# First self attention's scores as three 16 bit products instead of one 32 bit product, with new orders of the first and middle rounds, in a fused attention and feed-forward kernel on one Trainium2 core

## The reference, cut to what matters

```python
def _attention(q_in, k_in, v_in, WQ, WK, WV, causal):
    Q = einsum('bse,ed->bsd', q_in, WQ); K = einsum('bse,ed->bsd', k_in, WK); V = einsum('bse,ed->bsd', v_in, WV)
    scores = einsum('bqd,bkd->bqk', Q, K) / sqrt(d)       # causal: masked above the diagonal
    return einsum('bqk,bkd->bqd', softmax(scores), V)
...
a = _attention(inputs, inputs, inputs, Wq, Wk, Wv, causal=True) + inputs   # the "first attention"
h = _layer_norm(a, gamma, beta)
c = _attention(h, context, context, Wcq, Wck, Wcv, causal=False) + h       # over 257 context rows
h = _layer_norm(c, gamma, beta)
f = relu(einsum('bse,ed->bsd', h, W1) + b1)
return relu(_layer_norm(f + h, gamma, beta))
...
x = x + xattn(layernorm(x), ctx)          # block 1
x = x + attn16heads(layernorm(x))         # block 2
x = x + ffn(layernorm(x))                 # block 3: a gated feed-forward, and experts for some rows
```

## Time and profile before

| | us |
|---|---|
| median of 3 runs (1462.0 to 1462.47) | 1462.03 |
| the profiled execution's own time | 1461.23 |
| its span, first to last instruction | 1459.4 |
| PE busy | 1369.7 (94%) |
| DVE busy | 1128.3 (77%) |
| ACT busy | 588.8 (40%) |
| POOL busy | 529.0 (36%) |
| mean granted TensorE clock | 0.992 |
| a round in the middle (the same unit of one tile and the next, 703.08 to 743.92) | 40.84 |

### The profile page before, as it was taken

The page is one execution under the profiler, slowest core; times in us unless marked ns, Lnnn a source line. Parts: engine busy times, 40 slices in busy tenths (PEclk is TensorE's granted clock), DMA queues, the critical chain, the costliest instruction groups (busy, mean ns, idle before and its releaser), DMA issues.

```text
span 1459.4 us, 32980 instructions
## 1 busy us (share of the span) xinstructions
PE 1369.7 (94%) x13732; PEld 857.8 (59%) x13733; DVE 1128.3 (77%) x2334; ACT 588.8 (40%) x1115; POOL 529.0 (36%) x545
## 2 busy tenths in 40 slices
PE   7679999999999999999999999999999999999888
PEld 3345566666566666666666666656656566655443
DVE  5776687777887777777878778777778778777876
ACT  2543334344444444433444444444344444433232
POOL 0133334344343334434443333434433333433222
PEclk9899999999999999999999999999999999999999
DMA  9723444333334444323334444323323444323540
GB/s 349 256 82 122 145 146 141 112 112 127 110 128 146 145 146 145 127 99 131 112 115 145 146 146 146 136 100 121 131 102 139 146 145 146 142 87 152 191 176 30
DMA packets 38660, 201.39 MB, mean 138 GB/s; under 512 B 5096, under 2 KB 5992, under 8 KB 28400
## 3 DMA queue, kind: packets, MB, share of 16 engines
q1 hardware_dynamic: 37648, 198.93, 38.2%
q10 hardware_dynamic: 864, 0.36, 0.1%
HBM read 182.24 MB, written 17.04 MB: 137 GB/s over the span
## 4 chain that ended last, share of the span: by engine, by line
PE 70%; DVE 19%; ACT 4%; POOL 4%; issue 3%; DMA 0%; DVEq 0%; POOLq 0%; ACTq 0%; SPq 0%
PE ps_a L1703 11%; PE ps_a L1726 8%; PE ps_t L1726 8%; PE ps_a L1712 6%; PE ps_t L1690 6%; PE ps_a L1767 4%; PE ps_a L1738 4%; PE ps_v L1703 4%; PE ps_t L1703 3%; DVE stats L1165 3%; POOL rstd L629 3%; DVE arena L1296 3%; PE ps_t L1738 2%; PE ps_t L1759 2%; PE ps_t L1810 2%
## 5 line engine op out<-in xcount | busy, mean ns | idle before, releaser
L638 POOL TENSOR_TENSOR act_l<-act_t,act_h 128x512 f16<-128x512 f32 (+1 forms) x176 | 199.2, 1132 | 383.8 <-ACT act_t L782 221.9
L629 POOL TENSOR_TENSOR rstd<-var,mhalf 128x1 f32<-128x1 f32 x224 | 185.5, 828 | 302.8 <-DVE var L1167 302.7
L638 POOL TENSOR_TENSOR last_slot<-last_slot 128x512 f16<-128x512 f32 x80 | 89.5, 1119 | 167.7 <-ACT last_slot L782 96.8
L774 ACT ACTIVATE act_h<-ps_t,scale 128x512 f16<-128x512 f32 (+1 forms) x110 | 70.8, 643 | 156.2 <-PE ps_t L1690 156.2
L1726 PE MATMUL ps_a<-act_h,arena 128*128 128x128 f16 x1408 | 87.5, 221 | 18.0 <-ACT act_h L774 18.0
L1726 PEld LDWEIGHTS ps_a<-act_h,arena 128*128 128x128 f16 x1408 | 81.8, 99 | 28.3 <-ACT act_h L774 22.3
L1726 PE MATMUL ps_t<-act_h,arena 128*128 128x128 f16 x1408 | 88.0, 222 | 4.5 <-ACT act_h L774 4.5
L1726 PEld LDWEIGHTS ps_t<-act_h,arena 128*128 128x128 f16 x1408 | 82.4, 99 | 6.1 <-issue 2.9
L1703 PE MATMUL ps_a<-arena,act_h 128*128 128x512 f16 x352 | 83.4, 380 | 1.6 <-ACT act_h L774 1.6
L782 ACT ACTIVATE act_t<-ps_t,scale 128x512 f32<-128x512 f32 (+1 forms) x110 | 70.2, 639 | 34.9 <-PE ps_t L1690 34.9
L1296 DVE TENSOR_SCALAR arena<-ps_a,unscale 32x512 f32<-32x512 f32 x64 | 48.3, 754 | 43.7 <-PE ps_a L1738 42.5
(11 more groups left out here) (369 smaller groups left out, 3087.7 us busy)
## 6 DMA issues: line engine op xcount, KB each, us to landing
arena<-in_ctx_t SPq DMA_DIRECT2D x32, 2056.0 KB, 8.4
arena<-in_ctx_n SPq DMA_DIRECT2D x32, 2048.0 KB
ctx_last<-in_ctx_last SPq DMA_DIRECT2D x32, 256.0 KB
arena<-in_ew SPq DMA_DIRECT2D x8, 1024.0 KB, 6.2
x_in<-in_x SPq DMA_DIRECT2D x22, 256.0 KB, 7.2
x_scratch<-rows SPq DMA_DIRECT2D x22, 256.0 KB, 8.7
out<-rows SPq DMA_DIRECT2D x22, 256.0 KB, 2.0
arena<-in_ew SPq DMA_DIRECT2D x8, 512.0 KB, 7.5
```

The lines of the kernel that those rows point to most:

```text
L629: nc.gpsimd.tensor_tensor(rstd[s][:], var[s][:], mhalf[:], ALU.pow).then_inc(rstd_ready[s], 1)
L638: nc.gpsimd.tensor_tensor(act_l[s][:, chunks], act_t[s][:, chunks], act_h[s][:, chunks], ALU.subtract).then_inc(act_l_ready[s], 1)
L774: nc.scalar.activation(act_h[s][:, 0:width // P].rearrange("p c r -> p (c r)"), bank[s][:, 0:width], ACT.Copy, scale=scale[:, k:k + 1]).th ...
```

## The change

1. The scores become three 16 bit products. The queries are kept in `q_t`'s buffer as two 16 bit parts, `q_h` and `q_l`. ACT gets a new unit `project_self` that makes `q_h` from the bank with a fixed power of two. DVE's `project_self` then waits for it and makes `q_l`, the bank times that power less `q_h`. PE's `self_scores` makes, for each quarter, `q_h` by `act_h`, `q_h` by `act_l`, and `q_l` by `act_h`: twelve matmuls of 128x128x128 in 16 bit. It waits for `act_l` instead of `act_t`. The counts of `q_ready` grow from 3 to 4 a tile.
2. The scale is put right in DVE's `self_scores` by a new column `K_SELF`, made by one more small instruction in `set_02`.
3. `FIRST` and `ORDER` are replaced. `LAST` has ACT's new unit, and its starts and ends are moved over the round's edge; its order is else the same.

```diff
-K_WQK, ..., K_Y, K_PLAIN = range(13)
-NSCALE = 13
+K_WQK, ..., K_Y, K_PLAIN, K_SELF = range(14)
+NSCALE = 14
+SELF_TOP = 18
...
+            q_h = [flat_rows(q_t[s]).bitcast(F16)[:, 0:C * P] for s in SLOTS]
+            q_l = [flat_rows(q_t[s]).bitcast(F16)[:, C * P:2 * C * P] for s in SLOTS]
...
+                def project_self(s, r, tile):                      # ACT
+                    act.wait_ge(q_done[s], 3 * r + 1)
+                    nc.scalar.activation(q_h[s], ps_a[s][:], ACT.Copy, scale=2.0 ** -SELF_TOP).then_inc(q_ready[s], 1)
...
+                        step(nc.vector.tensor_scalar(unscale[:, K_SELF:K_SELF + 1], unscale[:, K_WQK:K_WQK + 1],
+                                                     2.0 ** (SELF_TOP - SCALED_TOP) * PLAIN_TOP, None, ALU.mult))
...
                 def project_self(s, r, tile):                      # DVE
-                    dve.wait_ge(q_done[s], 3 * r + 1)
-                    nc.vector.tensor_scalar(q_t[s][:].rearrange("p c r -> p (c r)"), ps_a[s][:],
-                                            unscale[:, K_WQK:K_WQK + 1], None, ALU.mult).then_inc(q_ready[s], 1)
+                    dve.wait_ge(q_ready[s], 4 * r + 1)
+                    nc.vector.scalar_tensor_tensor(q_l[s], ps_a[s][:], 2.0 ** -SELF_TOP, q_h[s], ALU.mult, ALU.subtract
+                                                   ).then_inc(q_ready[s], 1)
...
                 def self_scores(s, r, tile):                       # PE
-                    pe.wait_ge(q_ready[s], 3 * r + 1)
-                    pe.wait_ge(act_t_ready[s], 8 * r + 1)
+                    pe.wait_ge(q_ready[s], 4 * r + 2)
+                    pe.wait_ge(act_l_ready[s], 8 * r + 1)
                     for c in range(C):
-                        mm = nc.tensor.matmul(ps_a[s][:, 0:P], q_t[s][:, c, :], act_t[s][:, c, :],
-                                              start=(c == 0), stop=(c == C - 1))
+                        here = slice(c * P, (c + 1) * P)
+                        nc.tensor.matmul(ps_a[s][:, 0:P], q_h[s][:, here], act_h[s][:, c, :], start=(c == 0), stop=False)
+                        nc.tensor.matmul(ps_a[s][:, 0:P], q_h[s][:, here], act_l[s][:, c, :], start=False, stop=False)
+                        mm = nc.tensor.matmul(ps_a[s][:, 0:P], q_l[s][:, here], act_h[s][:, c, :], start=False,
+                                              stop=(c == C - 1))
```

More of the change, by code:

```diff
@@ L103 @@
+    "pool": [(2, "set_2"), (3, "turn_z"), (0, "xn_moments"), (1, "set_1"), (0, "turn_xn"), (2, "head_scores"),
+        (1, "turn_w"), (2, "head_mix"), (1, "context_out"), (1, "turn_h2"), (2, "project_out"), (0, "self_mix"),
+        (0, "turn_h"), (1, "hidden"), (2, "turn_x2n"), (1, "out_norm"), (1, "turn_x1n"), (2, "silu")],
 }
 ORDER = {
[L105 to L120, removed]
+    "pe": [(2, "project_q"), (3, "turn_z"), (2, "project_k_l"), (3, "ffn_out"), (3, "ffn_out_l"), (1, "turn_pc"),
+        (2, "project_q_l"), (1, "context_mix"), (2, "head_scores"), (0, "turn_xn"), (2, "project_v"),
+        (0, "project_self"), (0, "project_self_l"), (1, "turn_w"), (2, "project_v_l"), (1, "context_out"),
+        (0, "self_scores"), (1, "context_out_l"), (0, "value_self"), (0, "value_self_l"), (0, "turn_p"),
+        (2, "head_mix"), (0, "self_mix"), (2, "project_out"), (1, "turn_h2"), (2, "project_out_l"), (1, "hidden"),
+        (1, "hidden_l"), (0, "turn_h"), (2, "turn_x2n"), (0, "project_query"), (0, "project_query_l"), (2, "ffn_in"),
+        (0, "context_scores"), (2, "ffn_in_l"), (1, "turn_x1n"), (1, "project_k")],
@@ new lines @@
+    "dve": [(3, "z_norm"), (2, "project_k"), (3, "ffn_out"), (0, "xn_moments"), (1, "context_total"), (0, "turn_xn"),
+        (2, "head_scores"), (1, "context_mix"), (1, "context_scaled"), (2, "head_total"), (0, "project_self"),
+        (2, "head_weights"), (0, "self_scores"), (1, "context_out"), (1, "context_norm"), (0, "self_mix"),
+        (2, "project_out"), (0, "self_norm"), (2, "x2_norm"), (1, "hidden"), (1, "out_norm"), (1, "x1_norm"),
+        (2, "ffn_in"), (0, "context_scores"), (2, "silu")],
@@ L121 @@
+    "act": [(3, "turn_x2n_t"), (2, "turn_x1n"), (3, "ffn_in"), (2, "turn_x1n_t"), (3, "turn_z"), (3, "turn_z_t"),
+        (1, "context_scores"), (2, "project_k"), (1, "turn_pc"), (2, "project_q"), (0, "turn_xn_t"), (0, "turn_xn"),
+        (1, "context_sum"), (2, "head_scores"), (1, "context_scaled"), (0, "project_self"), (1, "turn_w"),
+        (1, "turn_w_t"), (0, "self_scores"), (2, "project_v"), (0, "value_self"), (0, "turn_p"), (2, "head_mix"),
         (2, "head_mix_t"), (1, "turn_h2"), (1, "turn_h2_t"), (0, "turn_h"), (0, "turn_h_t"), (2, "turn_x2n"),
```

80 lines of the change are left out of this document (44 added, 36 removed), and 9 rows, old and new, of the table FIRST.

## The result

The changed kernel takes **1452.43 us** (median of 4 runs, 1448.41 to 1455.46) against 1462.14 (1462.0 to 1462.47): ratio 0.9933, 95% interval [0.9919, 0.9947]. 1451.6 was forecast, within 1446 to 1458. So the sum was right. Two of its three terms were not, and they cancel (the table behind the experiments). The median also lies between two pairs of executions (1448.41 and 1449.59, 1455.27 and 1455.46), so that it came within 0.8 us of the forecast is in part luck.

A forecast was written before the change was run, and what follows sets the result against it. PE was taken to bound the middle, while in the first rounds PE waits and list order decides. -8 - 2.6 + 0.2 = -10.4 us on 1461.23 gave 1450.8, plus 0.8 for the median: 1451.6 us, range 1446 to 1458.

The forecast's parts named there:

- first rounds: Rounds 0 to 3: walking all engines through the new lists, PE waits get covered; 8 us won, bounds 0 to 12.
- middle: 26 repeating rounds of 40.84 us, each 0.10 shorter: 2.6 us won, bounds 0 to 5.7.
- last rounds: Final two tiles: DVE is tight and its scores part comes later; 0.2 us lost, plus or minus 1.
- The matmuls: PE's scores: twelve 16 bit matmuls at 55.6 ns take 0.67 us instead of 0.89, saving 0.22 a tile.
- The step is covered by `context_out`: PE's `context_out`, 1.74 us, placed ahead of the scores hides the new ACT and DVE step; uncovered it costs 0.4 a tile.
- The wait behind ACT's new unit, 0.12: ACT's new `project_self` delays the cast of `turn_w`, so PE's `context_out` waits 0.12 us a round.
- Slack of 0.2 at `head_mix`: ACT's `project_v`, now behind the exponential, ends 0.2 us before PE's `head_mix` needs it, the round's thinnest cover.
- the middle gives nothing: Rival, chance 0.14: `context_out` waits 0.22 or `head_mix` waits 0.1, so middle rounds gain nothing; 1454.2 us.
- slower: Rival, chance 0.06: ACT's two activations do not overlap, `context_out` waits 0.48, each middle round loses 0.26.
- the wide pitch: Rival, chance 0.02: weight loads of the twelve matmuls are not hidden, up to 111 ns a pair; 1473 us.
- The first rounds give little: Rival, chance 0.14: DVE, not PE, bounds the first rounds, so only 2 us are won there; 1457.6 us.
- More than the walk: Rival, chance 0.09: the clock stays up in round 1 and the middle keeps 0.2 a round; 1445 us.

The follow-up runs named there:

- e10: The changed kernel, unaltered, run and profiled a second time: 1448.87 us, ratio 0.9904.
- e6: The changed kernel with the scores put back ahead of `context_out` in PE's middle list: 1457.56 us, ratio 0.9964.
- e5b: The changed kernel with the factor of ACT's `project_self` read from a one-column tile instead of a constant: 1453.92 us, ratio 0.9937.
- e2: The kernel before with only the new orders, 32 bit scores and no ACT `project_self`: 1454.40 us, ratio 0.9952.
- e1: The kernel before with the three products in the old orders, ACT's new unit behind `context_scaled`: 1480.55 us, ratio 1.0128.
- e7: The changed kernel with only one of the three score products, high part by high part: 1445.68 us, ratio 0.9886.
- e8: The changed kernel with the old lists for the first four rounds and ACT's `project_self` behind `turn_w_t`: 1463.47 us, ratio 1.0007.
- e4: The changed kernel with PE's `e_turn`, `e_logits` and `e_in0` behind `context_out_l` in the last rounds: 1449.96 us, ratio 0.9923.
- e3: The changed kernel with the old lists for the first four rounds and ACT's `project_self` behind `context_scaled`: 1477.21 us, ratio 1.0104.

## Why the prediction was right, and where it was not

Spans, before minus after, for the profiled execution and for e10:

| term | forecast | profiled | e10 |
|---|---|---|---|
| first rounds (to tile 4) | 8 | 6.6 | 9.3 |
| middle (tile 4 to 29) | 2.6 | 5.5 | 5.5 |
| last rounds | -0.2 | -5.5 | -2.3 |
| sum | 10.4 | 6.6 | 12.5 |

- **The matmuls**: right. 0.67 us for twelve, 56 ns each, and the weight loads are hidden. The Trainium skill ("TensorE: Matmul & The Clock Gate", section "Back-to-back issue gap") gives 81 ns for a sustained pair; this stream does not agree, and matches the 56 ns that it gives for the isolated gap.
- **The step is covered by `context_out`**: right. e6 takes the cover away and loses 0.25 a round, not the 0.4 that I gave, as ACT's unit lasts 0.60 and not 0.69, and DVE's part 0.69 and not 0.73.
- **The wait behind ACT's new unit, 0.12**: this is the mis-sized term; it measured 0.02, which is worth 2.5 us over 25 rounds. I took duration and pitch from line 774, whose factor comes from a tile; line 812 has a constant. e5b gives it the tile's form and the round grows by 0.09, to 40.725, close to the 40.74 announced. The Trainium skill ("ScalarE: Activation LUTs", section "What ACT_TABLE_LOAD costs") has this: each operand read from a tile adds about 93 ns. The rows agree (0.69 and 0.60); I had not looked at the form of the operand. The rest of the middle's 5.5 is one round of before that lasts 41.18 (tile 14 to 15) and now 40.63, 0.34 more than the others; e2 has it too and e1 does not, so it goes with the 32 bit product. It arises in front of `turn_h`, where DVE is 0.35 late; why was not traced.
- **Slack of 0.2 at `head_mix`**: right in place and size, by e7. It was not used up.
- **First rounds**: right in size, but not where the walk had it, so the size is in part luck. At the first `project_k` the lead is 4.7 (5.8 in e10) and not 3.6: `turn_w:0` came 2.2 us earlier than the walk had it, although `turn_p` of round 1 then stands 3.68 us for its exponential, a wait that I did not list. From there to the `project_k` of 196.04 only 1.5 (3.1 in e10) are won, and not 5.4. One reason is that I doubled what I read from one stretch: the stretch ahead of it, 108.38 to 151.06, is 42.68 long and not 44.98. The other is that the four waits are covered as said, 2.58 together, but the new ones of 0.66, 0.31 and 1.15 take 2.12 back. Up to the `context_scores` of tile 4 another 0.4 is won. That the orders do it is shown by e2. What differs between 6.6 and 9.3 is the start and the clock, by e10.
- **Last rounds, -0.2**: the step that failed, beyond its bound of 1. Two causes. The first I had named and sized too small: DVE's scores part is late, `turn_p` waits 0.52 (row 1312.92), and each of the last three rounds is some 0.3 longer, 0.85 in all; with a wait for the exponential near the end that is 0.25 longer (1.46 against 1.21) it makes 1.1. e2, without the new step, has none of it; e1 and e8, with it, lose 1.2 there, and their matmuls behind `e_turn` last 1.03 and 5.38 as before. The second I had not looked for: the granted clock behind the idle time at `e_turn` and near the end, 1.2 us in e10 and 4.3 in the profiled execution (2.6 and 1.7). Why it stays low for longer in one execution than in another is open.
- **The rivals**: "the middle gives nothing" is excluded by 40.63, "slower" by the cast at 693.30, the wide pitch by 0.67. "The first rounds give little" is excluded by their 6.6 to 9.3. "More than the walk" had the middle right, at 0.205 a round, and the clock wrong. PE's busy time fell by 4.1 us in the profiled execution and by 8.5 in e10, where 7 was forecast: matmuls at the lower clock are busy for longer.
- **The median**: the eight executions of the changed kernel in both sets have a median of 1449.05, 2.6 below the forecast and inside its range.

Are the two parts of the change separable? No. Order alone gives 8.4 us of span, the arithmetic alone in old lists costs 18.7 (e1: 1478.1; by e8 some 12 of them are the place of ACT's unit in the first rounds), both together gave 6.6 and 12.5. In the middle, 0.015 gained and 0.045 lost become 0.205 gained: the shorter products pay only where the order covers the step that they need. Of the versions that keep all three products, e4 is the only one near the change's best, and it is no better than e10, so none here beats the change.

## What to carry to other kernels

Before taking a duration from a row, compare the operand forms too: the same engine, shape and types with a factor from a tile instead of a constant was 0.09 us longer, and in a chain that PE already waits for, that was most of the error of the middle. A step added to an engine that works through its list in order should first be priced by what is listed behind it: e3 and e8 differ by one unit's place and 12 us. Waits that a new order covers can come back at later units, as at 179.41 here, so a walk should list the waits of each whole round, and not only those that go. And where the end of a kernel has waits of 2 to 3 us on PE, run the unaltered kernel twice before crediting an edit there: two profiles of one kernel lay 5.9 us apart, and e4's gain was of that kind.

## What the runs showed of the hardware

- An ACT activation of 128x512 from PSUM: 0.60 us with the next 0.50 later with a constant factor, 0.69 and 0.58 with a factor from a tile.
- Pairs of 16 bit weight load and matmul of 128x128x128 in a run of twelve: 56 ns each, with matmuls directly before and behind.
- The lower clock costs at the same places in some executions and not in others, after waits of the same length: 32 matmuls of 128 columns 3.48 or 1.95 us, four others 3.62 or 1.96.
